# Experts of a mixture layer: four units of one tile with weights of their own among 32 units of two tiles, TensorE's program written out

## The reference, cut to what matters

```python
logits = flat @ gate_w.T                      # flat: 4096 x 256, gate_w: 8 x 256
top_vals, top_idx = jax.lax.top_k(logits, 2)
top_w = jax.nn.softmax(top_vals, axis=-1)
...
for e in range(8):
    hdn = jax.nn.gelu(flat @ w1[e] + b1[e])   # 256 -> 1024
    out = out + combine[:, e:e + 1] * (hdn @ w2[e] + b2[e])   # 1024 -> 256
```

## Time and profile before

| | us |
|---|---|
| median of 3 runs | 783.26 |
| the profiled execution | 781.53 |
| its span, first to last instruction | 779.7 |
| TensorE busy | 713.2 |
| VectorE busy | 440.9 |
| POOL busy | 407.9 |
| ScalarE busy | 331.9 |

### The profile page before, as it was taken

The page is one execution under the profiler, slowest core; times in us unless marked ns, Lnnn a source line. Parts: engine busy times, 40 slices in busy tenths (PEclk is TensorE's granted clock), DMA queues, the critical chain, the costliest instruction groups (busy, mean ns, idle before and its releaser), DMA issues.

```text
span 779.7 us, 18458 instructions
## 1 busy us (share of the span) xinstructions
PE 713.2 (91%) x5438; PEld 676.9 (87%) x5439; DVE 440.9 (57%) x1047; ACT 331.9 (43%) x640; POOL 407.9 (52%) x480
## 2 busy tenths in 40 slices
PE   5899999999948888489999999999999999999993
PEld 4899898998926666389999999999999999999993
DVE  3675756756636999735445455455454454454551
ACT  2673755747515677332323323323323223233230
POOL 1474565787662443273555546546555555555233
PEclk9999999999969999599999999999999999999997
DMA  7759568497460333224557536665576276273122
GB/s 243 247 174 398 208 264 359 163 333 252 171 271 28 111 110 109 84 75 120 170 156 229 178 55 206 186 176 148 155 246 166 41 237 175 48 229 77 19 29 30
DMA packets 45873, 130.14 MB, mean 167 GB/s; under 512 B 5185, under 2 KB 35521, under 8 KB 41217
## 3 DMA queue, kind: packets, MB, share of 16 engines
q1 hardware_dynamic: 30560, 104.86, 36.3%
q0 software_dynamic: 13904, 19.45, 14.6%
q10 hardware_dynamic: 1360, 5.24, 1.7%
HBM read 186.80 MB, written 47.59 MB: 301 GB/s over the span
## 4 chain that ended last, share of the span: by engine, by line
PE 55%; issue 1%; DMA 0%; POOL 0%; DVE 0%; ACT 0%; POOLq 0%; DVEq 0%
PE ps_h L73 9%; PE ps_h L74 9%; PE ps_h L75 9%; PE ps_y L73 8%; PE ps_y L75 8%; PE ps_y L74 8%; PE ps_x L1596 2%; PE ps_y L1589 1%; DMA out_tok<-y,to_row 0%; POOL out_tok L1471 0%; DVE xtl L1531 0%; DVE yb L1551 0%; DVE y L1558 0%; ACT xth L1496 0%; POOL to_row L1467 0%
## 5 line engine op out<-in xcount | busy, mean ns | idle before, releaser
L1505 ACT ACTIVATE g<-ps_h,bias 128x256 f32<-128x256 f32 x288 | 120.8, 471 | 277.7 <-PE ps_h L75 277.7
L1471 POOL DMA_INDIRECT out_tok<-y,to_row x72 | 126.9, 1763 | 137.7 <-DVE y L1558 117.2
L73 PE MATMUL ps_h<-xth,wbuf 128*128 128x256 f32 x576 | 163.2, 283 | 3.3 <-issue 1.8
L73 PE MATMUL ps_y<-wbuf,gl 128*128 x576 | 164.6, 286 | 0.0
L74 PE MATMUL ps_h<-xtl,wbuf 128*128 128x256 f32 x576 | 163.1, 283 | 0.0
L75 PE MATMUL ps_h<-xth,wbuf 128*128 128x256 f32 x576 | 161.8, 281 | 0.0
L75 PE MATMUL ps_y<-wbuf,gh 128*128 x576 | 161.7, 281 | 0.0
L74 PE MATMUL ps_y<-wbuf,gh 128*128 x576 | 161.7, 281 | 0.0
L73 PEld LDWEIGHTS ps_h<-xth,wbuf 128*128 128x128 f32 x576 | 108.0, 188 | 3.7 <-issue 2.1
L75 PEld LDWEIGHTS ps_h<-xth,wbuf 128*128 128x128 f32 x576 | 109.6, 190 | 0.0
L74 PEld LDWEIGHTS ps_y<-wbuf,gh 128*128 128x128 f32 x576 | 108.8, 189 | 0.0
(11 more groups left out here) (239 smaller groups left out, 1284.9 us busy)
## 6 DMA issues: line engine op xcount, KB each, us to landing
wbuf<-wsplit SPq DMA_DIRECT2D x71, 2048.0 KB, 8.1
wsplit<-wbuf SPq DMA_DIRECT2D x14, 2048.0 KB, 11.9
wraw<-in_w SPq DMA_DIRECT2D x16, 1024.0 KB, 7.9
raw<-in_x_ch ACTq DMA_DIRECT2D x5, 1024.0 KB, 8.8
normed<-x SPq DMA_DIRECT2D x8, 528.0 KB, 3.0
tok<-in_x_tok SPq DMA_DIRECT2D x1, 4096.0 KB, 16.7
out_tok<-tok SPq DMA_DIRECT2D x8, 512.0 KB, 3.7
x_rows<-normed,from_row POOLq DMA_INDIRECT x72, 3.4
```

Source lines behind the costliest of these rows:

```text
L73: eng.matmul(out, ll, rh, start=first, stop=False)
L1471: pool.indirect_dma_start(out=out, out_offset=bass.IndirectOffsetOnAxis(ap=to_row[:, par, s:s + 1], axis=0), in_=y[:, par, s, :], in_offse ...
L1505: last = act.activation(g[:, f, :], ps_h[:, q, f % 2, :], ACT.Gelu_apprx_tanh, bias=bias1[:, bass.ds(e, 1), f:f + 1].rearrange("p a f -> p ...
```

## The change

The number of full pairs of an expert becomes (count + 127) >> 8, at least 1: a remainder of more than 128 rows gets a pair, one of 1 to 128 rows a lone tile. In every period of eight units the last (7, 15, 23 and 31) is a lone unit: 128 rows, of any expert that has a lone tile, with weights from a third buffer `lone_w` (4 MB). So 36 usual units are now 32 pairs and 4 lone ones. If there are more pairs than 32 or more lone tiles than 4, a further run of ten full units follows (`PAIRS` is 46). SP loads the lone weights in quarters of 1 MB in the units 0 to 3 of each period. Because a lone unit may be of expert 0 or 1, stage B writes their second layers to `wsplit` (two DMAs of 2 MB). To make room, `x`, `g`, `y` and `yb` are put where stage B's tokens were. POOL's iota of the unit numbers becomes three. VectorE begins stage C with `lone_table`. All engines loop over eight units in place of four, except TensorE, whose 37 steps are written out. For lone units ScalarE, VectorE and TensorE work on 128 rows; gathers and scatters still move two tiles. TensorE's unit orders are otherwise the same.

```diff
-PAIRS = 2 * TOK // PAIR + E - 1
-USUAL = 2 * TOK // PAIR + E // 2
+PERIOD = 8
+LONE = PERIOD - 1
+LONES = E // 2
+FULL = 2 * TOK // PAIR
+USUAL = FULL + LONES
+FULL_TOP = FULL + E - 2
+PAIRS = FULL_TOP + E
+REST = FULL_TOP + LONES
...
@@ stage B, SP, ahead of the load of bias2 @@
+            for e in range(2):
+                sp.dma_start(wsplit[e, :, W2AT:WROW], wbuf[:, e, W2AT:WROW].bitcast(F32)).then_inc(second_out, 16)
...
@@ stage B, POOL @@
-                    (expert_id[:, :], [[1, E]], 0, 0), (place0[:, :], [[CAP, E]], 0, 0), (tile_id[:, :], [[1, PAIRS]], 0, 0),
+                    (expert_id[:, :], [[1, E]], 0, 0), (place0[:, :], [[CAP, E]], 0, 0),
+                    (by_period[:, :, 0:LONE], [[LONE, LONES], [1, LONE]], 0, 0),
+                    (by_period[:, :, LONE], [[LONE, LONES]], LONE - 1, 0),
+                    (tile_id[:, LONES * PERIOD:REST], [[1, REST - LONES * PERIOD]], LONES * LONE, 0),
...
@@ stage B, make_table @@
-                then(dve.tensor_scalar(count_i[:, :], ps_count, float(PAIR - 1), None, ALU.add))
+                then(dve.tensor_scalar(count_i[:, :], ps_count, float(P - 1), None, ALU.add))
...
@@ stage C @@
-        def steps(eng, body, lo, hi, end):
+        def steps(eng, body, lo, hi, end, written_out=False):
             u = lo
-            if hi == USUAL:
+            if hi == USUAL and not written_out:
                 start = lo + SLOT
-                loops = (hi - LEAD - start) // SLOT
+                loops = (hi - LEAD - start) // PERIOD
...
+        def alone(u, at):
+            return at % PERIOD == LONE and not (isinstance(u, int) and u >= USUAL)
+        def rows_of(u, at):
+            return P if alone(u, at) else PAIR
...
@@ stage C, SP @@
+            def lone_weights(u, at):
+                layer, n = at // 2, W2AT // 2
+                e = entry(sp, T_EXPERT, u + (LONE - at), E - 1)
+                cols = slice(at * n, (at + 1) * n)
+                sp.dma_start(lone_w[:, cols].bitcast(F32),
+                             wsplit[bass.ds(e, 1)].rearrange("a p w -> (a p) w")[:, cols]).then_inc(lone_in[layer], 16)
...
+                    if at < 4 and not (isinstance(u, int) and u + LONE - at >= USUAL):
+                        lone_weights(u, at)
...
@@ stage C, VectorE, ahead of the first x_low @@
+            def lone_table():
...
+                extra = USUAL - LONES * PERIOD
+                dve.tensor_tensor(in_periods(tabs[:, T_CHANGED, :])[:, 1:LONES, 1], in_periods(pair_experts[:, :])[:, 1:LONES, 1],
+                                  in_periods(pair_experts[:, :])[:, 0:LONES - 1, LONE - 2], ALU.is_gt)
...
+                then(dve.tensor_scalar(lone_tiles_i[:, :], count_i[:, :], P.bit_length() - 1, None, ALU.arith_shift_right))
+                then(dve.tensor_copy(lone_tiles[:, :], lone_tiles_i[:, :]))
...
+                for i in range(1, PAIRS - USUAL + 1):
+                    then(dve.tensor_scalar(buffer_f[:, i:i + 1], buffer_f[:, i - 1:i], -1.0, 1.0, ALU.mult, ALU.add))
+                dve.tensor_copy(tabs[:, T_BUFFER, USUAL:PAIRS], buffer_f[:, 1:PAIRS - USUAL + 1]).then_inc(lone_set, 1)
...
@@ stage C, TensorE @@
-            def layer1(u, slot):
-                par = slot % 2
-                wh, wl = [wbuf[:, par, i * W2AT // 2:(i + 1) * W2AT // 2].rearrange("p (k n) -> p k n", k=KT) for i in range(2)]
+            def layer1(u, at):
+                par, n = at % 2, rows_of(u, at)
+                both = lone_w[:, 0:W2AT] if alone(u, at) else wbuf[:, par, 0:W2AT]
+                wh, wl = [both[:, i * W2AT // 2:(i + 1) * W2AT // 2].rearrange("p (k n) -> p k n", k=KT) for i in range(2)]
...
+                if alone(u, at):
+                    pe.wait_ge(lone_in[0], periods(u, at) * 32 + 32)
...
-                            last = mm3(pe, ps_h[:, q, f % 2, :], (wh[:, k, rows], wl[:, k, rows]),
-                                       (xth[:, par, k], xtl[:, par, k]), k == 0, k == KT - 1)
+                            last = mm3(pe, ps_h[:, q, f % 2, 0:n], (wh[:, k, rows], wl[:, k, rows]),
+                                       (xth[:, par, k, 0:n], xtl[:, par, k, 0:n]), k == 0, k == KT - 1)
...
-                for s in range(2):
+                for s in range(rows_of(u, at) // P):
...
-                steps(pe, body, lo, hi, hi)
+                steps(pe, body, lo, hi, hi, written_out=True)
```

More of the change, by code:

```diff
@@ L694, in _, with stage_b @@
             images(pe, image)
-def stage_b(nc, sem, tok, wbuf, wsplit, ident, fixed, xn, tabs, bias1, bias2, records, normed, b1_t, b2, out):
+def stage_b(nc, sem, tok, wbuf, wsplit, ident, fixed, xn, tabs, bias1, bias2, records, count_i, n_pairs, ends,
+            expert, expert_id, normed, b1_t, b2, out):
     with ExitStack() as ctx:
@@ L743, in stage_b @@
         empty = sb("empty", [P, CELLS])
[L745 to L749, removed]
+        pairs_i = sb("pairs_i", [P, E], I32)
+        past, picked = sb("past", [P, REST, E]), sb("picked", [P, REST, E])
+        passed, starts, first = sb("passed", [P, REST]), sb("starts", [P, REST]), sb("first", [P, REST])
+        expert_i = sb("expert_i", [P, REST], I32)
         ps_out = ps("ps_out", [P, B, HALF])
@@ L1190, in make_table @@
                 dve.memset(tabs[:, T_CHANGED, 0:1], 0)
                 dve.tensor_scalar(tabs[:, T_CHANGED, 1:2], expert[:, 1:2], 0.0, None, ALU.is_gt)
[L1192 to L1196, removed]
+                dve.tensor_tensor(tabs[:, T_CHANGED, 2:REST], expert[:, 2:REST], expert[:, 0:REST - 2], ALU.is_gt)
@@ L1198, in decode @@
+                then(dve.tensor_copy(expert_i[:, :], expert[:, 0:REST]))
+                dve.tensor_scalar(tabs[:, T_BUFFER, 0:REST], expert_i[:, :], 1, None, ALU.bitwise_and)
+                then(dve.scalar_tensor_tensor(out=tabs[:, T_FIRST, 1:REST], in0=expert[:, 1:REST], scalar=float(E - 1),
+                                              in1=first[:, 1:REST], op0=ALU.is_lt, op1=ALU.mult))
             def decode():
@@ L1322, with stage_c @@
 T_EXPERT, T_COLUMN, T_FIRST, T_NEXT, T_BUFFER, T_TOTAL, T_CHANGED = range(7)
-def stage_c(nc, sem, wbuf, ident, tabs, bias1, bias2, records, wsplit, normed, out):
+def stage_c(nc, sem, room, wbuf, ident, tabs, bias1, bias2, records, count_i, n_pairs, ends, pair_experts, expert_id,
+            wsplit, normed, out):
     with ExitStack() as ctx:
@@ L1394, in entry, with before, loads_of_first_layer @@
             return eng.value_load(tabs[0:1, row, bass.ds(u, 1)], min_val=0, max_val=top)
[L1396 to L1402, removed]
+        def before(u, at):
+            return u // SLOT if isinstance(u, int) else (u - at % SLOT) // SLOT
+        def loads_of_first_layer(u, at):
+            return before(u, at) * (SLOT // 2) + (at % SLOT + 1) // 2
         block = ctx.enter_context(nc.Block())
@@ L1440, in run @@
                 sp.wait_ge(w2_in, (hi - 1) * 16)
+                if lo == 0:
+                    for s in lone_in:
+                        sp.wait_ge(s, LONES * 32)
             all_pairs(sp, run)
@@ L1504, in hidden @@
                     for f in (2 * q, 2 * q + 1):
[L1505 removed]
+                        last = act.activation(g[:, f, 0:n], ps_h[:, q, f % 2, 0:n], ACT.Gelu_apprx_tanh,
                                               bias=bias1[:, bass.ds(e, 1), f:f + 1].rearrange("p a f -> p (a f)"))
@@ L1530, in x_low, with keep_share @@
+            def x_low(u, at):
+                par, n = at % 2, rows_of(u, at)
                 dve.wait_ge(xh_d, done(u))
-                dve.tensor_tensor(xtl[:, par], ps_x[:, :, :], xth[:, par].bitcast(F32), ALU.subtract).then_inc(xl_d, 1)
-            def keep_share(u, slot):
+                dve.tensor_tensor(xtl[:, par, :, 0:n], ps_x[:, :, 0:n], xth[:, par, :, 0:n].bitcast(F32), ALU.subtract
+                                  ).then_inc(xl_d, 1)
+            def keep_share(u, at):
+                slot = at % SLOT
@@ L1556, in result @@
                 dve.wait_ge(share_d, done(u))
-                for s in range(2):
+                for s in range(m):
                     last = dve.tensor_scalar(y[:, par, s, :], yb[:, s, :], share[:, slot, s:s + 1], None, ALU.mult)
```

222 lines of the change are left out of this document (152 added, 70 removed).

## The result

Three runs of the changed kernel took 773.88, 773.98 and 771.36 us (median 773.88), against 783.26 before: 0.987 of it, with a 95% interval of 0.985 to 0.989, so 9.4 us less. A further six runs beside runs of the kernel before (the first experiment) gave 0.9865, 0.984 to 0.989: 10.6 us less by this ratio and 12.0 by the medians (771.65 against 783.64). The forecast was 769.7 us, 13.6 less. The direction and the mechanism held; 4 us of the gain did not arrive in the first three runs, and 1.6 to 3 in the six.

A forecast was written before the change was run, and what follows sets the result against it. TensorE's work in the expert stage was taken as the bound: -14.0 us from four lone units, +0.2 table, +0.2 iotas make -13.6, off the median of 783.26 gives 769.7 us; range 765.5 to 779 us.

The forecast's parts named there:

- What bounds the kernel: Expert stage, from about 329 us: TensorE busy 300.00 of 300 us between 400 and 700 us; only its work or waits count.
- How many units are short: Expert stage: 32 pairs and four lone tiles in place of 36 pairs, 68 tiles computed in place of 72.
- What a lone unit saves: TensorE, per lone unit: second layer 2.86, transposes 0.22, first layer 0.43 us; 3.5 us in sum, 14.0 for four.
- Nothing ends later for it: After a lone unit's short second layer, about 1 us of cover is left; cost nothing, 0.5 us each if it fails.
- the sign for it: TensorE trace of the expert stage: four gaps of 8.3 us between blocks of transposes, among gaps of 11.87.
- Start of the stage: Start of expert stage: VectorE's lone table, 7.1 us, just fits into 8.33 us idle, cost 0.2; two more POOL iotas, 0.2.
- The expert program written out, cost 0: TensorE's straight code in the expert stage: taking the loop away saves nothing and instructions do not run short; 0 us.
- rival C: Expert stage: half the gain lost to waits behind lone units, late weights or late instructions; 776 us, up to 781; chance 0.08.
- The tail stays as it is: End of the kernel, after the last product at 760.85 us: unchanged, since the last four units are pairs.
- A: Lone first layers: fp32r products of 128 columns cost like fp32, 0.22 us each; slower, 790.9 us; chance 0.13.
- B: Lone first layers: faster pace of 0.08 us a product, 5.0 us saved a unit, 764 us; chance 0.05.
- D: Unit counts: one pair or lone tile too many, so TensorE runs ten extra units, 119 us; chance 0.01.

The follow-up runs named there:

- the first experiment: The changed kernel run again without any edit, beside the kernel before: 0.9865 of the kernel before (0.984 to 0.989), median 771.65 us.
- The 64-column run: The changed kernel with only 64 columns moving in the first layer of lone units, half their rows not computed: its one execution took 782.6 us.

## Why the prediction was right, point by point

- **What bounds the kernel.** TensorE in the expert stage, with no gap from unit 2 on, before and after. Right.
- **How many units are short.** 32 pairs and four lone ones, no overflow (576 - 64 and 64 products per line). Right.
- **What a lone unit saves.** Forecast 3.5 us, measured 3.37: second layer 2.83 (forecast 2.86), first layer and transposes 0.54 (forecast 0.65, with a pace of 0.110 that is 0.112). The step that decided, the pace of products of 128 columns, was rightly read off the nearest row, the stage's own transposes. The 64-column run shows that the columns do not set it, which leaves the load of the weights. The Trainium skill's 81 ns for a stream of 128 columns ("TensorE: Matmul & The Clock Gate", Back-to-back issue gap) does not hold for fp32r here, at 112. The same page's section on LDWEIGHTS gives columns over 1.2 GHz, an estimate of 107 ns for 128 columns; that is near the measured 112 at the full clock, but at the half clock the products were 210 apart.
- **Nothing ends later for it.** Right for lone units, weights and gathers; no wait of TensorE between units 2 and 35. Only the sign for it was put wrongly: 8.3 us in one block, where the same saving lies in two.
- **Start of the stage.** The table is hidden, by 0.9 us; it takes 6.3 us (330.18 to 336.49 in the repeated profile) for 7.1 forecast. The two iotas cost 0.3 (the mask waits 3.49 us in place of 3.18). From the copy of stage A to the first transposes it is 0.7 us more than before in the first profile and 0.4 in the repeated one, for 0.4 forecast.
- **The expert program written out, cost 0.** The number held and the argument compared the wrong things. Written out against the old loop of four is nothing (1.0004). But a period of eight units leaves only a loop of eight to compare with, and that costs 13.4 us. So the sentence that taking the loop away saves nothing was true and missed that keeping it was not free: the gain of the lone units and the written-out program are one edit. The Trainium skill's rule on taken branches ("Runtime: NRT & Kernel Launch", Instruction fetch mechanics) was cited and then put down to rival C since the trace of before shows no stall. That trace could not show one, since its loop of four units is hardly fetched again; the loop of eight does what the rule says. For the other engines the forecast held: POOL, VectorE, ScalarE and SP loop over eight units, q14 has 9 packets between 400 and 700 us in place of 3, and TensorE never waits for them.
- **The tail stays as it is.** This is the step that failed. "The tail after 760.85 us stays as it is, since the last four units are pairs" looked at the units and not at the code behind them: ten units in place of three stand behind the condition, and the branch over them costs 2.5 us on the path that sets the end. It is the largest part of the 4 us.
- **The rest.** From -13.6 forecast: 0.5 less saved by lone units, up to 0.3 more in stage B and 2.5 in the tail make -10.3, and blocks without anything lone are 11.84 us in the mean where they were 11.86, with which the stage is about 0.8 shorter: -11.1 us. The spans of the kernel before and of the repeated changed kernel are 11.2 us apart (779.7 and 768.5), and the six runs of the first experiment stand at -10.6 by the ratio and -12.0 by the medians. The first three runs, at -9.4, had the late load and the clock in their profile.
- **The rivals.** A (fp32 speed for 128 columns), B (0.08 us) and D (extra units) are refuted by the pace and the counts. C's 776 us lay 2.1 us above the first median and 4.4 above the second, and its place is wrong: nothing waits behind lone units.

Open: why the plain units are a little shorter. Before, their blocks alternate between 11.82 and 11.90 us; in the changed kernel most take 11.83 or 11.84, and 11.89 stands only ahead of the lone units and once in the first units. It is not the written-out program, which has 11.86 in the mean on the kernel before, while a loop with the change has 11.83 in most blocks; the buffers lie elsewhere in memory since, but nothing was run on that.

## What to carry to other kernels

A unit of half the rows saves in the product where the rows are stationary, not where they move and every product brings its own 128x128 weights: there 64 and 128 columns had the same pace, and going from 256 to 128 saved 6% of the time. Where a loop's period must grow, count what its body becomes in TensorE's instructions before comparing it with the loop that was; here four units looped for free, eight stalled 4 to 5 us at each branch back and then lost 2 us to the clock, and straight code was the form that cost nothing at eight units. Code that never runs is not free at the end of a kernel: put the branch over it ahead of the last wait.

## What the hardware showed that was not expected

- A TensorE loop of four units (some 400 products) moved 2 instruction packets in 300 us; one of eight (some 800) moved 26 and stalled 4.07 to 4.88 us at each branch back.
- The granted clock fell from 2.4 to 1.2 GHz while TensorE issued back to back, with products of 64 columns (0.112, then 0.21 us apart), in all four lone units of one execution. With 128 columns at the same pace it stayed at 1.00.
- A taken branch over ten units of code instead of three made the end of the kernel 2.5 us longer behind a finished DMA, and cost nothing when taken before it landed. Two instruction packets after the landing go with the longer end.
